# A one-core decoder layer: first keys before first values, one context product moved into the prologue, and the last expert blocks in pairs

## The reference

```python
# attention (16 heads of 16); ctx is (8, 128, 256)
cq  = layernorm(xn @ W_dq);  ckv = layernorm(xn @ W_dkv)
K_nope, V = split(ckv @ W_ukv)          # 224 columns of keys, 256 of values
x = x + softmax(mask(q @ k.T)) @ V @ W_o.T

# cross attention (2 heads of 128)
Q, K, V = xn @ Wh, ctx @ Wh, ctx @ Wh   # V is the "context product"
A = maximum(abs((Q @ K.T * decay).sum(axis=0)), 1)   # summed over the 8 sequences
x = x + (relu(xn @ wg) * groupnorm(A @ V)) @ wo

# experts: each token goes to its two best of 16, and to the shared expert
y = sum_k weight_k * (silu(xn @ gate[e_k]) * (xn @ up[e_k])) @ down[e_k]
y = y + (silu(xn @ shared_gate) * (xn @ shared_up)) @ shared_down
x = x + y
```

## Time and profile before

| what | value |
|---|---|
| median of 3 runs | 240.82 us (240.66 to 242.6) |
| the profiled execution's own time | 240.65 us |
| its span in the profile | 238.8 us |
| PE busy | 226.9 us (95%) |
| DVE busy | 143.7 us (60%) |
| ACT busy | 123.0 us (51%) |
| POOL busy | 80.0 us (33%) |
| share of PE in the chain that ended last | 75% |
| granted TensorE clock | 1.00 (2.4 GHz) in every stretch asked |

### The profile page before, as it was taken

One profiled execution on the slowest core, in us unless ns is written; L12 is line 12 of the kernel. 1 busy time (PEld: TensorE's weight loads), 2 busy tenths in 40 slices (PEclk: granted clock), 3 DMA queues, 4 the chain that ended last, 5 costly groups with the idle time before them and its releaser, 6 DMA issues.

```text
span 238.8 us, 5442 instructions
## 1 busy us (share of the span) xinstructions
PE 226.9 (95%) x1808; PEld 158.0 (66%) x1808; DVE 143.7 (60%) x442; ACT 123.0 (51%) x444; POOL 80.0 (33%) x95
## 2 busy tenths in 40 slices
PE   8977899999999999999999999999999999999992
PEld 6534567666676776889878878784555556556561
DVE  1568988979888778352989558976232322222181
ACT  2136998989898888924142620612333334333220
POOL 2221131111121101010375100266577777754152
PEclk9999999999999999999999999999999999999999
DMA  6999977600002800000601300013693333696683
GB/s 198 278 349 350 339 165 165 146 26 1 4 0 57 290 3 0 3 1 7 237 0 44 131 3 0 5 47 100 162 315 102 110 91 100 186 311 183 188 297 133
DMA packets 20638, 30.62 MB, mean 128 GB/s; under 512 B 2361, under 2 KB 15299, under 8 KB 20611
## 3 DMA queue, kind: packets, MB, share of 16 engines
q1 hardware_dynamic: 17603, 23.34, 32.7%
q0 software_dynamic: 2304, 6.29, 8.9%
q10 hardware_dynamic: 704, 0.64, 0.9%
HBM read 25.02 MB, written 5.24 MB: 127 GB/s over the span
## 4 chain that ended last, share of the span: by engine, by line
PE 75%; DVE 12%; DMA 3%; issue 2%; POOL 2%; ACT 2%; SPq 1%; DVEq 0%; ACTq 0%; POOLq 0%
PE bank L966 12%; PE bank L983 8%; PE bank L891 6%; PE bank L632 6%; PE bank L589 5%; PE bank L619 4%; PE bank L644 3%; PE bank L566 3%; PE bank L663 3%; PE bank L955 3%; PE bank L717 3%; PE bank L945 2%; DMA bxT<-in_wh_t 2%; PE bank L595 2%; PE bank L601 2%
## 5 line engine op out<-in xcount | busy, mean ns | idle before, releaser
L1100 ACT ACTIVATE pr_s<-bank,mx 128x128 f32<-128x128 f32 x128 | 45.4, 387 | 7.4 <-DVE mx L1336 7.4
L551 POOL DMA_INDIRECT expert_out<-by,prT x24 | 26.5, 1104 | 18.0 <-ACT by L1090 14.4
L1670 DVE COPY bxT<-bank 128x256 f32<-128x256 f32 x24 | 10.1, 423 | 37.2 <-PE bank L968 35.6
L966 PE MATMUL bank<-gu_s,bxT 128*64 x96 | 31.2, 466 | 0.0
L1090 ACT ACTIVATE prT<-bank 128x512 f32<-128x512 f32 (+1 forms) x56 | 27.5, 513 | 3.2 <-PE bank L644 2.0
L1100 ACT ACTIVATION_READ_ACCUMULATOR pr_s<-bank,mx 128x1 f32 x128 | 28.9, 226 | 0.0
L546 POOL DMA_INDIRECT qx_s<-ffn_in,prT x24 | 23.5, 978 | 14.3 <-issue 8.5
L1336 DVE TENSOR_REDUCE mx<-bank 128x4 f32<-128x512 f32 x32 | 21.2, 685 | 4.6 <-PE bank L619 4.6
L983 PE MATMUL bank<-dn_s,prT 88*64 x96 | 22.9, 379 | 0.4 <-ACT prT L1090 0.4
L891 PE MATMUL bank<-ck_s,sgu_s 128*128 128x256 f32 (+1 forms) x96 | 22.3, 382 | 0.0
L1255 ACT ACTIVATE pr_s<-bank 128x176 f32<-128x176 f32 x24 | 7.6, 318 | 27.1 <-PE bank L968 27.1
(11 more groups left out here) (206 smaller groups left out, 477.2 us busy)
## 6 DMA issues: line engine op xcount, KB each, us to landing
gu_s<-in_w_gu SPq DMA_DIRECT2D x8, 704.0 KB, 7.3
dn_s<-in_w_dn SPq DMA_DIRECT2D x4, 704.0 KB
early<-in_w_gu SPq DMA_DIRECT2D x8, 352.0 KB, 4.5
early<-in_w_dn SPq DMA_DIRECT2D x8, 176.0 KB
gu_s<-in_ctx_in SPq DMA_DIRECT2D x2, 512.0 KB, 9.6
ffn_in<-x_s SPq DMA_DIRECT2D x4, 256.0 KB, 2.5
cv_s<-expert_out SPq DMA_DIRECT2D x4, 256.0 KB, 3.3
x_s<-expert_out SPq DMA_DIRECT2D x4, 256.0 KB, 5.6
```

The costliest lines, as they stand in the source:

```text
L551: pool.indirect_dma_start(expert_out[:], bass.IndirectOffsetOnAxis(ap=idx[:, 1, k:k + 1], axis=0), by[:, k % RB, :], None).then_inc(dma_sc ...
L966: mm(bank[2 + i % 2][0:HT, 0:2 * I], bxT[:, i % 2, k, 0:HT], gu_s[:, k, bass.ds(e, 1), :], start=k == 0, stop=k == KD - 1, skip_group_chec ...
L1100: last = nc.scalar.activation(pr_s[:, n % 2, h, :], score_bank(n)[:, h * T:(h + 1) * T], ACT.Exp, bias=mx[:, n % 4, h:h + 1], accum_out=de ...
```

## The change

Five edits, all of order and of buffers; no product, copy or transfer of the computation is added or dropped.

1. **First keys.** For tile 0 only, the 480-column product is split. The keys (224 columns) go first, into `bank[7]`, with their own semaphores `pe_first_keys` and `act_first_keys`; the values follow in `bank[3]`. `qk_transpose(0)` waits for the copy of the keys alone.
2. **Context product.** `ctx_values(0, 0)` moves from the end of the attention to the prologue, behind `qk_transpose(0)`, in `bank[2]`. Its copy on ACT moves with it, between `kv_out(0)` and `latents_out(1)`. `ctx_values(1, 0)` keeps `bank[1]` and waits for `act_exp`, and `ctx_values(0, 1)` stands before `cross_scores(4)`.
3. **Dummy products.** Three more before `wh_square`, two more before `queries(0)`.
4. **The last four blocks.** `expert_up(21)` returns to the loop, and the end works in pairs 20, 21 and 22, 23. `shared_up(3, 1)` and `shared_up(3, 2)` are cut into their two halves, which stand between the pairs' steps. ACT and DVE follow the same order, and `shared_silu(3, 2)` comes behind `y_out(23)`.
5. **The way out.** SP issues the read of `yg[t]` for t of 3 and more only when `yg[t - 3]` has landed. On DVE the two sums of tile 0 stand ahead of `shared_mul(3, 2)`, the other ten behind it.

```diff
+            def first_keys_values():
+                for k in range(2):
+                    last = mm(first_key_bank[:, 0:NOPE], ckvT[:, 0, k, :], wkv_s[:, k, 0:NOPE], start=k == 0, stop=k == 1)
+                last.then_inc(pe_first_keys, 1)
+                for k in range(2):
+                    last = mm(bank[3][:, NOPE:NOPE + D], ckvT[:, 0, k, :], wkv_s[:, k, NOPE:NOPE + D], start=k == 0, stop=k == 1)
+                last.then_inc(pe_keys_values, 1)
...
             weight_mean()
+            keep_busy(bank[7], 3)
             wh_square()
...
             ctx_keys(0, 1)
+            keep_busy(bank[7], 2)
             pe.wait_ge(ld_w_q, 16)
             pe.wait_ge(ld_w_kv, 16)
             queries(0)
-            keys_values(0, 0)
-            keys_values(0, 1)
+            first_keys_values()
             qk_transpose(0)
+            ctx_values(0, 0)
             latent_transpose(1)
...
             for t in range(B):
+                if t >= 3:
+                    sp.wait_ge(dma_token_outputs[t - 3], 16)
                 sp.dma_start(yg[t].rearrange("p k d -> p (k d)"),
...
             hidden_transpose(last - 3)
-            expert_up(last - 2)
+            hidden_transpose(last - 2)
+            shared_up(PAIRS - 1, 1, (0,))
             expert_down(last - 3)
-            pe.wait_ge(dve_block_T, last)
-            shared_up(PAIRS - 1, 1)
-            hidden_transpose(last - 2)
+            expert_down(last - 2)
             expert_up(last - 1)
             expert_up(last)
-            expert_down(last - 2)
-            shared_up(PAIRS - 1, 2)
+            shared_up(PAIRS - 1, 1, (1,))
             hidden_transpose(last - 1)
             hidden_transpose(last)
+            shared_up(PAIRS - 1, 2, (0,))
             expert_down(last - 1)
             expert_down(last)
+            shared_up(PAIRS - 1, 2, (1,))
...
-            shared_mul(PAIRS - 1, 2)
-            weigh_pair(0)
+            shared_mul(PAIRS - 1, 1)
+            dve.wait_ge(dve_shared_added, PAIRS - 1)
+            weigh(0, 0)
+            weigh(0, 1)
+            shared_mul(PAIRS - 1, 2)
+            weigh(1, 0)
+            weigh(1, 1)
             weigh_pair(2)
```

More of the change, by code:

```diff
@@ L316, in decoder_layer @@
         ctx_key_bank = lambda g, h: bank[6 if g else h]
-        ctx_value_bank = lambda g, j: bank[1 + j]
+        ctx_value_bank = lambda g, j: bank[1 if g and not j else 2]
+        first_key_bank = bank[7]
         rden_half = lambda b: bank[6 if b < B - 1 else 5][:, D:2 * D]
@@ L598, in qk_transpose @@
                 pe.wait_ge(dve_queries, b + 1)
-                pe.wait_ge(act_keys_values, b + 1)
+                pe.wait_ge(act_keys_values, b + 1) if b else pe.wait_ge(act_first_keys, 1)
                 for k in range(4):
@@ L700, in ctx_values @@
             def ctx_values(g, j):
-                if g == 0:
+                if (g, j) == (0, 0):
                     pe.wait_ge(ld_wh, 16)
-                    pe.wait_ge(act_probs_T, NC * B - 2) if j else pe.wait_ge(act_exp, NC * B - 1)
+                elif g == 0:
+                    pe.wait_ge(act_probs_T, NC * B - 2)
                 else:
-                    pe.wait_ge(act_ctx_values, j + 1)
+                    pe.wait_ge(act_ctx_values, 2) if j else pe.wait_ge(act_exp, NC * B - 1)
                 for u in range(2):
@@ L811, in _ @@
             cross_transpose(B - 2)
-            ctx_values(0, 0)
+            ctx_values(0, 1)
             cross_scores(4)
             cross_scores(5)
-            ctx_values(0, 1)
             cross_scores(6)
@@ L1055, in _ @@
                 expert_up(i)
-                if i + 4 < BLOCKS:
-                    expert_up(i + 1)
+                expert_up(i + 1)
                 expert_down(i - 2)
@@ L1104, in kv_out @@
             def kv_out(b):
+                if b == 0:
+                    act.wait_ge(pe_first_keys, 1)
+                    copy(qk[:, 0, D:D + NOPE], first_key_bank[:, 0:NOPE]).then_inc(act_first_keys, 1)
                 act.wait_ge(pe_keys_values, b + 1)
@@ L1109, in kv_out @@
                     act.wait_ge(pe_weighed, NC * (b - 2))
-                copy(qk[:, b % 2, D:D + NOPE], bank[3][:, 0:NOPE])
+                if b:
+                    copy(qk[:, b % 2, D:D + NOPE], bank[3][:, 0:NOPE])
                 copy(v_s[:, b % 3, :, 0:VB - DH].rearrange("p a (h e) -> p a h e", h=8)[:, :, :, 0:DH],
@@ L1165, in _ @@
             kv_out(0)
+            ctx_values_out(0, 0)
             latents_out(1)
@@ L1276, in _ @@
                 silu(i)
-                if i + 4 < BLOCKS:
-                    silu(i + 1)
+                silu(i + 1)
                 y_out(i - 2)
@@ L1281, in _ @@
             hT_out(last - 3)
-            silu(last - 2)
+            hT_out(last - 2)
             y_out(last - 3)
-            shared_silu(PAIRS - 1, 1)
-            hT_out(last - 2)
+            y_out(last - 2)
             silu(last - 1)
             silu(last)
-            y_out(last - 2)
-            shared_silu(PAIRS - 1, 2)
+            shared_silu(PAIRS - 1, 1)
             hT_out(last - 1)
@@ L1293, in _ @@
             y_out(last)
+            shared_silu(PAIRS - 1, 2)
             act.wait_ge(dve_shared_added, PAIRS + 1)
@@ L1676, in h_mul, with weigh @@
                 V.tensor_tensor(bh[:, i % 2, :], bank[2 + i % 2][:, I:2 * I], bs[:, i % 2, :], ALU.mult).then_inc(dve_hidden, 1)
+            def weigh(u, k):
+                dve.wait_ge(dve_first_sum, u + 1) if k else dve.wait_ge(dma_token_outputs[u], 16)
+                V.scalar_tensor_tensor(x_s[:, u, :], yg[u][:, k, :], top_w[k][:, u:u + 1], x_s[:, u, :],
+                                       ALU.mult, ALU.add).then_inc(dve_second_sum if k else dve_first_sum, 1)
             def weigh_pair(t):
-                dve.wait_ge(dve_shared_added, min(t // 2 + 1, PAIRS - 1))
                 for k in range(2):
                     for u in (t, t + 1):
-                        dve.wait_ge(dve_first_sum, u + 1) if k else dve.wait_ge(dma_token_outputs[u], 16)
-                        V.scalar_tensor_tensor(x_s[:, u, :], yg[u][:, k, :], top_w[k][:, u:u + 1], x_s[:, u, :],
-                                               ALU.mult, ALU.add).then_inc(dve_second_sum if k else dve_first_sum, 1)
+                        weigh(u, k)
             def diagonals():
@@ L1707, in _ @@
                 h_mul(i)
-                if i + 4 < BLOCKS:
-                    bT_out(i + 3)
-                    h_mul(i + 1)
-            h_mul(last - 2)
-            bT_out(last)
-            shared_mul(PAIRS - 1, 1)
+                bT_out(i + 3)
+                h_mul(i + 1)
             h_mul(last - 1)
             h_mul(last)
+            shared_mul(PAIRS - 1, 1)
+            dve.wait_ge(dve_shared_added, PAIRS - 1)
+            weigh(0, 0)
+            weigh(0, 1)
             shared_mul(PAIRS - 1, 2)
-            weigh_pair(0)
+            weigh(1, 0)
+            weigh(1, 1)
             weigh_pair(2)
```

2 lines of the change are left out of this document (1 added, 1 removed).

## The result

The changed kernel takes 238.7 us (median of 4 runs, 238.32 to 239.19) where the kernel before takes 241.2 us (median of 4, 240.66 to 242.6). The ratio is 0.9899, with a 95% interval of 0.9858 to 0.994: 1.0% faster. The forecast was 239.2 us, 0.7% faster. The profiled executions took 240.65 us before (span 238.8) and 238.32 us now (span 236.5), 2.33 us less.

What follows compares the result with a forecast made beforehand. PE, busy 95% of the span, was taken as the bound, so only its idle moments could be won: 240.65 - 0.75 (prologue) - 0.68 (attention) - 0.1 (end) = 239.12, stated as 239.2 us, range 238.0 to 240.7.

Steps and rivals of the forecast that it cites:

- within 1%: Whole kernel: the changed time differs from the time before by no more than 1%; chance 0.75.
- faster: Whole kernel: the change wins over 1%, a time under 238.4 us; chance 0.20.
- First keys: Prologue: copying tile 0's keys first starts its transposes and the masks 0.95 us earlier.
- Dummies: Prologue: three dummies before `wh_square` delay `front_project(0)` by 0.2 us (0.15 to 0.35); two before `queries(0)` cost nothing.
- Context product: End of the attention: one product less on full PE wins 0.68 us (0.5 to 0.89), limited by `cross_transpose(7)` waiting for DVE.
- The last blocks on PE and DVE: End: pairs save PE 0.75 us; shared down products near 228.9, DVE's ten sums from 229.68, last additions done at 234.52.
- DVE takes over as the bound: End: ten sums behind the last shared half make DVE the limit, leaving 0.1 us of PE's 0.75 us.
- Reads: End: first read at 223.65, three landings of about 2.8 us each, `yg[7]` at 232.7; PE waits 0.4 us.
- rival 1: End: held reads landing in 3.3 us each end the kernel 0.9 us later than before, total 240.1 us; chance 0.15.
- the wait before the last products is over a microsecond: End: PE's wait there, forecast as a few tenths, would prove the prediction wrong if this long.
- last sign: End: prediction wrong if the time from block 20's scatter to the end shrinks by much more than 1 us.
- Rival 4: End: DVE's sums hold block 23's scatter until 234.6, as before; if additions hold it too, 239.7 us; chance 0.05.

Runs made afterwards that it cites:

- experiment 10: The changed kernel measured again, unaltered, beside the combined run on the same chip: 238.89 us, ratio 0.9914.
- experiment 3: The changed kernel without SP's wait for `yg[t - 3]`, all eight reads issued one behind the other: 237.95 us, ratio 0.987.
- experiment 4: The changed kernel with one added wait: POOL issues block 23's scatter only when DVE's twelve sums are done: 240.07 us, ratio 0.996.
- experiment 8: The changed kernel without its five new dummy products: 238.98 us, ratio 0.9892.
- experiment 7: The kernel before with the first keys alone, no dummy products added and no context product moved: 239.85 us, ratio 0.9943.
- experiment 2: The kernel before with only the held reads, reordered sums and last blocks in pairs; its front is the old one: 240.63 us, ratio 0.9958.
- experiment 1: The kernel before with only the first keys, context product and dummy products; its end is the old one: 239.16 us, ratio 0.9919.
- experiment 5: The changed kernel without the wait for reads, and with both sums of tile 1 also ahead of the last shared product: 237.91 us, ratio 0.9857.
- experiment 6: The changed kernel without the wait for reads, reads issued in the order 0, 1, 2, 6, 3, 7, 4, 5: 238.18 us, ratio 0.9862.
- experiment 9: The changed kernel without the wait for reads, tile 1's sums ahead, block 20 finished first so reads start earlier: 237.22 us, ratio 0.9858.

## Why the prediction was right, and where it failed

The sign and the size were right: 239.2 us was forecast and 238.7 measured, inside the range; the ratio of 0.9899 lies on the edge between "within 1%" (0.75) and "faster" (0.20). The steps of the front hold, and the end failed in two steps that nearly cancel: the reads, and POOL.

**First keys: right.** Forecast 0.95 us, measured 0.99 from `front_project(0)` to the masks, in the changed kernel and in six of the seven other profiles with all edits of the front (10.51 or 10.52, against 11.50; 10.72 in experiment 10). `qk_transpose(0)` starts 8.64 us after `front_project(0)` where it was 9.61, 0.97 us earlier. `queries(1)` just held, as argued: the row stands at 19.33 with no wait of PE, 1.21 us earlier than before.

**Dummies: right for the profile of before, less on average.** I took 0.2 us. In experiments 3 and 4, where `weight_mean` took 2.41 us as in the profile of before, `front_project(0)` starts at 7.70 and 7.78, 0.11 and 0.19 us later than 7.59. Over all eight profiles the mean start is 7.62, so the mean cost is nearer to nothing. The 0.3 us for which PE idled there depend on when `weight_mean` ends and when the load lands, and both vary, as experiment 8 shows. The masks start at 18.16 on average over eight profiles, 0.93 us earlier than before, where 0.75 was forecast; the 1.20 us of the changed kernel's own profile hold some 0.2 of luck.

**Context product: right.** Forecast 0.68 us; 93.55 became 92.86, and 92.86 to 92.90 in six of the seven other profiles with all edits of the front (93.31 in experiment 10, where PE waited 0.7 us at the first product of a later tile, L570, where it mostly waits 0.3; experiment 8, without dummies, has the same wait and 93.27). Experiment 7, which has the first keys alone, keeps 93.54.

**The last blocks on PE and DVE: right.** Put 1.87 us later, to stand in the frame of before (POOL's first gather of rows starts at 156.61 there and at 154.74 now), the shared expert's down products start at 228.94 (forecast 228.9), block 22's scatter starts at 227.91 (forecast 227.8), block 23's at 229.19 (229.0), the ten sums at 229.90 (229.68), the first read at 223.74 (223.65). That DVE takes over as the bound was true only once the wait was gone: in experiment 3 the sums and additions end, in that frame (its first gather is 1.48 us earlier), at 234.67; the forecast was 234.52.

**Reads: the mechanism right, its size not.** I wrote three landings "at about 2.8 us each" and a wait of PE of 0.4 us. The three hops took 2.65, 2.77 and 4.37 us: the last one had the reads of `yg[4]` and `yg[5]` beside it, as I had counted, and also block 23's scatter, issued at the same moment, and SP's first stores of the output, which I had not. Whether these made it long is not shown: the read of `yg[6]` took 3.3 us in experiment 4, which has no scatter beside it, but 3.1 us in experiment 8 and 4.1 in experiment 10, which have one. The three hops average 3.26 us, which is rival 1's 3.3.

PE waited 2.0 us. That is rival 1 (given 0.15): its mechanism decided the changed kernel's chain, and its price, "0.9 us later than before", fell short of the 1.51 us that the stretch from `cross_mix` to the last addition lost. That loss is itself one draw: in the four other profiles with held reads it is 1.00, 1.01, 1.96 and 2.62 us (experiments 2, 4, 8 and 10; 0.7 us of the 1.96 came before the first read, and 0.95 of the 2.62 from the clock), and 0.1 us in experiment 3 without the wait.

The prediction also read its ceiling low: the 5.9 us of the earlier trace rows are the median of two reads, and the last of the eight took 6.1 us and landed at 232.0, not 231.7. By the prediction's own sign of an error ("the wait before the last products is over a microsecond") this step is wrong. Its last sign, that the time from block 20's scatter to the end shrinks by much more than 1 us, came out between: it shrank by 1.6 us (18.64 to 17.06) where the forecast's own terms make 1.15.

**POOL: the step that failed.** Rival 4 said of block 23's scatter that it "is caught until 233.73 + 0.85 = 234.6. It was done at 234.61 before, so nothing changes". Two things in it are wrong. It was not caught: issued 0.71 us ahead of the sums, it ran its 0.97 us through, also the last 0.26 us beside them. And its end in the kernel before was not without effect. It was the last thing that the kernel's end waited for, 4.2 us behind, and that stood in the profile of before: 234.61 and 238.8, with the last addition 4.59 us from the end. I carried this distance along as a constant. It became 2.67, and with it 1.92 us of the 2.33 came from an engine that I had given no term. (Rival 4's own time was off as well: a scatter done at 235.4 is 0.8 us later than 234.61, which makes 240.65 - 1.43 + 0.8 = 240.0, not 239.7.) Experiments 1, 4 and 7 keep or restore POOL's late end and have the 4.2 us; in 2, 3, 5, 6, 8, 9 and 10 POOL was done by 230.1, and SP's last wait is 0.2 us.

Rival 4 rested on the 3.85 us, in which a scatter that began *amid* the sums was held through all of them; I extended that to one that begins ahead of them. In the runs every scatter begun ahead took 0.96 or 0.97 us: in the changed kernel and in experiments 2, 3, 5, 6, 8, 9 and 10. The Trainium skill's page "SBUF — State Buffer" (section "SBUF: two separate sides") says of a VectorE instruction with two inputs in SBUF and a GpSimd instruction that reads SBUF that whichever starts first has the shared ports for its whole instruction, and that the other is blocked. (Whether the scatter is such an instruction no run here tells.) The trace agrees with half of it: block 23's scatter ran through. But the sums were not blocked by it. The first began 0.34 us after the start of the last `shared_mul`, and the first six took 2.57 us, both beside the end of the scatter; in experiment 4, with no scatter there, it is the same 0.34 and 2.57 us.

**The sum.** Forecast: 0.75 + 0.68 + 0.1 = 1.53 us. Profiled pair: 1.20 + 0.69 - 1.51 + 1.92 = 2.30 of 2.33; the missing 0.03 lies within the rounding of the spans to 0.1 us. The last two terms give 0.41 where I had 0.1; they hold errors of 1.6 and 1.9 us, and a forecast that is right by their near balance is right partly by chance.

## What to carry to other kernels

Work out what the last instruction of *every* engine and queue is, not just of the chain that the profile prints: here a scatter on POOL for which no read waited set the end from 4.2 us away, and having it 0.7 us ahead of VectorE's sums rather than behind them was worth 1.9 us, as much as the front's edits together. A wait that limits transfers in flight turns their landings into a chain: here the stretch to the last addition lost 1.0 to 2.6 us, from one profile to the next. Count it with the landings under the traffic that stands beside the last one, not with those at the start, and count what TensorE's clock may lose in the pause. When two bounds lie within half a microsecond of each other, do not expect a gain from one alone: each gave nothing that could be measured (experiments 5 and 6). Experiment 9 relieved both, and its profile is another 0.5 us shorter, but its ratio is that of experiment 5, so that the two together give more stays unproven.

## What the runs showed of the hardware

- From the end of POOL's last scatter to the end of the span it was 4.2 us in each of the four profiles where it ended last (before, experiments 1, 4 and 7: 4.19, 4.23, 4.20, 4.21, with spans printed to 0.1 us). For about 2.0 us SP waits for the landing; the rest is SP's last wait of 1.9 to 2.1 us, which is 0.2 us where POOL was done early. What it waits for is the `DRAIN` of POOL's queue: in these four profiles it ended 4.0 us after the end of the last scatter and 0.2 us before the end of the span. In the eight others it ended 4.8 to 6.2 us after the last scatter, 0.8 to 4.5 us before the end. What POOL does in it stays open.
- TensorE's clock fell to half in one of the five profiles in which it idled 1.1 to 2.0 us for held reads just ahead of its last products (experiment 10, after 1.79 us: 0.52, and 2.05 us for products of 1.10), and stayed at 1.00 in the four others, one of which had idled 2.00 us.
- A scatter begun while VectorE adds two operands from SBUF was held until 0.85 us after the last of twelve sums, 3.85 us in all; one begun 0.7 us ahead of them took 0.97 us, and so did one beside additions that read PSUM. The sums that began beside the last 0.26 us of a scatter were not slowed (2.57 us for the first six, with and without it).
- The four records of `weight_mean` (330 columns), at a granted clock of 1.00, took from 1.28 us (experiment 2) to 2.44 us (experiment 7) from one profile to the next. The cause stays open; the load that follows hides part of it.
